# Four layers of attention and feed-forward: the two halves of the transposed scores exchanged, and the values matmuls moved up behind turns and projections

## The reference

```python
xn = _layernorm(x)
s = attention_l(xn, Wq, Wk, Wv, Wo)     # 32 heads of 16
g = _silu(ffn_l(xn, ...))
x = x + s * g
```

## Time and profile before

| | us |
|---|---|
| median of 3 runs (lowest, highest) | 1302.31 (1296.14, 1303.39) |
| the profiled execution | 1305.54 |
| its span, first to last instruction | 1303.8 |
| TensorE busy in it | 1166.5 (89%) |
| VectorE busy | 846.7 (65%) |
| ScalarE busy | 643.0 (49%) |
| GpSimd busy | 475.2 (36%) |

### The profile page before, as it was taken

One profiled execution on the slowest core, in us unless ns is written; L12 is line 12 of the kernel. 1 busy time (PEld: TensorE's weight loads), 2 busy tenths in 40 slices (PEclk: granted clock), 3 DMA queues, 4 the chain that ended last, 5 costly groups with the idle time before them and its releaser, 6 DMA issues.

```text
span 1303.8 us, 22325 instructions
## 1 busy us (share of the span) xinstructions
PE 1166.5 (89%) x8476; PEld 864.2 (66%) x8476; DVE 846.7 (65%) x1362; ACT 643.0 (49%) x1122; POOL 475.2 (36%) x636
## 2 busy tenths in 40 slices
PE   3999998988989898889999999998888888897897
PEld 3788876765656555555678787777666666675574
DVE  7743468876766656664655556537887778676453
ACT  3334357565454645544233433337756565565653
POOL 1000127454321111212444434406754465545542
PEclk9999989999999999959999999999999999999897
DMA  7000010110001000010243222201001001010001
GB/s 259 1 1 1 1 34 2 49 60 2 2 2 36 2 1 2 26 50 26 73 146 97 81 89 73 73 33 51 3 2 41 2 3 34 2 47 2 2 26 40
DMA packets 15260, 48.06 MB, mean 37 GB/s; under 512 B 2858, under 2 KB 6959, under 8 KB 14388
## 3 DMA queue, kind: packets, MB, share of 16 engines
q1 hardware_dynamic: 15156, 46.63, 10.6%
HBM read 44.00 MB, written 2.10 MB: 35 GB/s over the span
## 4 chain that ended last, share of the span: by engine, by line
PE 65%; DVE 14%; ACT 12%; issue 6%; DMA 1%; POOL 0%; POOLq 0%; ACTq 0%; DVEq 0%; SPq 0%
PE bank L662 18%; PE bank L778 14%; PE bank L692 8%; PE bank L906 8%; ACT probs L1364 6%; PE bank L881 5%; DVE negmax L1795 3%; PE bank L795 3%; PE bank L829 2%; ACT pv L1374 2%; PE bank L861 1%; PE bank L809 1%; DMA W_lo_whole<-in_w 1%; DVE stats L1452 1%; DVE W_lo_whole L1577 1%
## 5 line engine op out<-in xcount | busy, mean ns | idle before, releaser
L1795 DVE TENSOR_REDUCE negmax<-bank 128x4 f32<-128x1024 f32 (+1 forms) x256 | 250.1, 1016 | 89.1 <-PE bank L838 64.2
L1364 ACT ACTIVATE probs<-bank 128x1024 f32<-128x1024 f32 (+1 forms) x256 | 211.1, 863 | 33.1 <-PE bank L861 28.2
L2022 POOL TENSOR_SCALAR_AFFINE_SELECT probs<-probs 128x512 f32<-128x512 f32 x192 | 125.6, 673 | 122.6 <-ACT probs L1364 121.7
L1991 POOL TENSOR_TENSOR scaled<-pvT,recip 128x128 f32<-128x128 f32 x128 | 56.1, 439 | 289.1 <-DVE recip L1823 286.2
L1947 POOL TENSOR_TENSOR W_lo<-W_lo_whole,W_hi 128x1536 fp32r<-128x1536 f32 x28 | 98.4, 3517 | 117.2 <-ACT W_hi L1116 117.2
L829 PE MATMUL bank<-kT,qT 64*128 64x256 f32 (+1 forms) x1024 | 105.9, 302 | 25.1 <-DVE negmaxT L1813 10.3
L881 PE MATMUL bank<-probs,V 128*32 128x256 f32 (+1 forms) x2048 | 121.6, 356 | 3.1 <-DVE negmax L1795 1.7
L861 PE MATMUL bank<-qT,kT 64*128 64x256 f32 (+1 forms) x640 | 114.8, 388 | 6.0 <-DVE h_lo_whole L1623 3.1
L1374 ACT ACTIVATE pv<-bank 128x256 f32<-128x256 f32 x128 | 49.2, 384 | 135.5 <-PE bank L881 135.3
L829 PEld LDWEIGHTS bank<-kT,qT 64*128 64x128 f32 x1024 | 86.4, 194 | 44.2 <-issue 18.5
L1116 ACT ACTIVATE W_hi<-W_lo_whole 128x1536 fp32r<-128x1536 f32 x28 | 41.7, 1488 | 136.4 <-DVE W_lo_whole L1577 136.4
(11 more groups left out here) (203 smaller groups left out, 2697.1 us busy)
## 6 DMA issues: line engine op xcount, KB each, us to landing
W_lo_whole<-in_w SPq DMA_DIRECT2D x28, 768.0 KB, 4.2
Wqkv_lo_whole<-in_Wqkv SPq DMA_DIRECT2D x6, 768.0 KB, 6.5
Wo_lo_whole<-in_Wo SPq DMA_DIRECT2D x4, 1024.0 KB, 4.9
Wqkv<-in_Wqkv SPq DMA_DIRECT2D x2, 1536.0 KB, 7.3
Wdown_whole<-in_Wd SPq DMA_DIRECT2D x1, 2816.0 KB, 14.8
x<-in_x SPq DMA_DIRECT2D x4, 512.0 KB, 5.7
out<-x SPq DMA_DIRECT2D x8, 256.0 KB, 2.0
V_lo_whole<-in_V SPq DMA_DIRECT2D x1, 1408.0 KB, 6.5
```

What stands on the lines that cost most here:

```text
L1364: nc.scalar.activation(A[l].probs[gi % 2][kb][:, :, q0 - kb * A[l].probs1:].rearrange("p (b h) q -> p b h q", b=2), B.tensor(key)[:, :, 0: ...
L1795: v.tensor_reduce(A[l].negmax[u % 2][:, qb, :].rearrange("p (b h) -> p b h", b=2)[:, :, 2 * g:2 * g + 2], B.tensor(key)[:, :, 0:2 * nk].re ...
L2022: gp.affine_select(out=blk, in_=blk, compare_op=ALU.is_ge, fill=0.0, base=0, pattern=[[0, 4], [1, P]], channel_multiplier=-1).then_inc(cau ...
```

## The change

1. In each slot half 1 of the transposed scores comes first on TensorE, then the rows scores, then half 0. ScalarE takes the exponentials of half 1 first, GpSimd cuts half 1 first.
2. `QKV_BANK` becomes 6, so turned queries and projections use the banks of half 1; grouped keys go to bank 4 (shared with the rows scores), the values to bank 3 (shared with half 0) and, in the last slots of a run, to bank 6 in place of 4.
3. The values matmuls stand directly behind turns, projections and first feed-forward chunks, ahead of tile turns, output products, `turn_max`, `group_values`, `tile1` and `down`. Before, they closed every slot that had a filler.

```diff
-QKV_BANK = 2
-KEYS_BANKS = {True: (7, 1), False: (4, 2)}
+QKV_BANK = 6
+KEYS_BANKS = {True: (4, 1), False: (4, 2)}
 def values_bank(U, g):
-    return 6 if U + 2 + g % 2 < RUN else 4
+    return 3 if U + 2 + g % 2 < RUN else 6
 def scores_cols(l, u, g, kb):
-    if g == 0 and kb == 0:
+    if g == 0 and kb == 1:
         pe.wait_ge(m_rows[u % 2], 32 * (4 * l + u // 2 + 1))
 def slot(r, G):        # TensorE
-    scores_cols(l, u, g, 0)
+    scores_cols(l, u, g, 1)
     if G + LEAD < RUN * GROUPS:
         scores_rows(r, G + LEAD, 0)
         scores_rows(r, G + LEAD, 1)
-    scores_cols(l, u, g, 1)
+    scores_cols(l, u, g, 0)
...
-    if G >= 1 and not filled_out:
+    if G >= 1:
         weigh_values(r, G - 1, G)
     if tile_turned(U, g) is not None:
         transposes(2 * r + 1, (tile_turned(U, g),), banks=(NORM_BANK,))
     for n in rows_projected(r, U, g):
         project_out(*n, 1 if U % 2 == 1 else (4, 5)[n[2]])
...
-    if G >= 1 and filled_out:
-        weigh_values(r, G - 1, G)
 def slot(r, G):        # ScalarE
-    exponentials(r, G, 0)
     exponentials(r, G, 1)
+    exponentials(r, G, 0)
 def cut_future(r, G):  # GpSimd
-    for kb in range(2):
+    for kb in (1, 0):
```

More of the change, by code:

```diff
@@ L873, in weigh_values @@
                 else:
-                    pe.wait_ge(*B.emptied(("ST", l, u, g, 1)))
+                    pe.wait_ge(*B.emptied(("ST", l, u, g, 0)))
                 for tau in range(2):
@@ L915, in slot @@
                     scores_rows(r, G + LEAD, 1)
-                scores_cols(l, u, g, 1)
-                filled_out = False
+                scores_cols(l, u, g, 0)
                 if g == 0 and U + 1 < RUN:
                     turn_stacks(*unit(r, U + 1), 1)
-                    filled_out = True
                 if g == 2 and U + 2 < RUN:
                     turn_stacks(*unit(r, U + 2), 0)
-                    filled_out = True
                 if g % 2 == 1 and U + 3 < RUN:
                     project(*unit(r, U + 3), g // 2, QKV_BANK)
-                    filled_out = True
                 if r == 0 and (U, g) in PART2_SLOTS:
@@ L994, in ffn0 @@
                 turn_max(0, 0, 6)
-                turn_stacks(0, 1, 0)
+                turn_queries(0, 1, 0, 2)
+                turn_keys(0, 1, 0, 7)
                 scores_rows(0, GROUPS, 0, (4, 2))
@@ L1383, in slot @@
                 U, g = divmod(G, GROUPS)
+                exponentials(r, G, 1)
                 exponentials(r, G, 0)
-                exponentials(r, G, 1)
                 if g == 0 and U + 1 < RUN:
@@ L2162, in loads_0 @@
                 if U == 15:
-                    sp.wait_ge(*B.filled(("ST", 1, UNITS - 2, GROUPS - 1, 1)))
+                    sp.wait_ge(*B.filled(("ST", 1, UNITS - 2, GROUPS - 1, 0)))
                     load_chunk(2)
@@ L2191, in slot @@
                 if r == 0 and (U, g) == (15, 3):
-                    sp.wait_ge(*B.filled(("ST", 1, UNITS - 1, GROUPS - 1, 1)))
+                    sp.wait_ge(*B.filled(("ST", 1, UNITS - 1, GROUPS - 1, 0)))
                     load_chunk(3)
@@ L2215, in _ @@
                 slot(1, G)
-            sp.wait_ge(*B.filled(("ST", 3, UNITS - 1, GROUPS - 1, 1)))
+            sp.wait_ge(*B.filled(("ST", 3, UNITS - 1, GROUPS - 1, 0)))
             load(b2_whole[:], a["b2"], ffn3_in[2])
```

## The result

The kernel became slower: 1322.37 us, median of 4 runs (1318.60 to 1323.25), against 1299.22 (1288.94 to 1303.39) for the kernel before on the same chip, ratio 1.0192 with a 95% interval of 1.0152 to 1.0233. The forecast was 1307 in a range of 1291 to 1319: the side was missed too, since "within 0.5%" had the largest chance. The profiled execution took 1322.69 us, its span 1320.9, at a mean granted clock of 0.962; the other three runs had 0.961 to 0.966. Over all experiments the kernel before ran 84 times, median 1298.7, with a mean clock of 0.973 (0.963 to 0.987).

What follows compares the result with a forecast made beforehand. The prediction took TensorE, busy 89%, to be bound by its waits in the slots, chiefly for exponentials. Gains of 12.4 us and costs of 16.9 made net +4.5 on a median of 1302.3: 1306.8, say 1307, range 1291 to 1319.

Steps and rivals of the forecast that it cites:

- The exchange in plain causal units: Causal slots, short half first: gain of 0.2 us for g 2 and 3, 0.3 for g 0 and 1; 3.5 in all.
- The waits for exponentials: TensorE before turned queries (L795) and projections: waits fall from 21.4 to about 8 us and 23.0 to about 10.
- The chain behind the product at g 2: Product, residual, copy of maxima, rows scores all later: that wait grows from 10.3 to 18 us or more, near 1.4 in (3, 3).
- `tile1`: Layer 1, values ahead of this filler: tanh and gate lose their cover, six slots 0.6 us later, cost 3.6 (0 to 5).
- `group_values`: Layer 1, values ahead of this filler: first scale operation 1.0 us later, 0.54 reaches TensorE in three slots, cost 1.6.
- Layer 1's exchange: Layer 1, order of halves: both have 1024 columns, so the first exponential ends at the same time; gain 0.
- The turned keys in bank 4: Causal slots: keys wait for the first row maximum, which was said to be mostly done by then; no cost given.
- The costs of layer 1: Values ahead of small fillers there: `tile1` 3.6 us, `group_values` 1.6, tile turns at bank 5 1.0; 10.7 by the reflection's count.
- Values ahead of an output product, g 0: Causal units: the projection starts at 240.0 instead of 240.49, 0.6 us gained in each of 9 slots, 5.6 (3 to 6).
- Values ahead of an output product, g 2: Product ends later, so the next projection is mostly 0.7 us later a slot; cost 6.2 us (3 to 8).
- rival C: Idle over 1.4 us behind g 2 output products and `tile1` brings the lower clock: eight dips add 12 us, 1319; chance 0.17.
- B: Rival: VectorE and ScalarE waits hide half the costs (8.5 us arrive), some 7 of half-clock time returns; 1292, chance 0.23.

Runs made afterwards that it cites:

- e1: Changed kernel with the values matmuls back at the end of every slot that has a filler (exchange of halves and banks alone): 1293.1 us, ratio 0.9965.
- e2: Kernel before with the values matmuls moved early in every slot, halves and banks as before: 1323.8 us, ratio 1.0212.
- e7: Kernel before with one unused VectorE operation (0.65 us) added ahead of the copy of the turned maxima, g 2 of units 3, 5, 7: 1298.2 us, ratio 1.0004.
- e5: Changed kernel with the maxima turned ahead of the output product and copied ahead of the residual: 1318.7 us, ratio 1.0154 to the kernel before.
- e6: e1 with the values of each run's last slots in bank 4, as in the kernel before, not bank 6: 1291.4 us, ratio 0.9952.
- e8: e6 with the maxima turned ahead of the output product and copied ahead of the residual: 1281.6 us, ratio 0.9845.
- e9: e8 with bank 6 for the values of unit 13 of run 0 alone: 1282.3 us, ratio 0.9842.
- e11: Changed kernel with values early only in units 8 to 15 of run 0 (layer 1), late everywhere else: 1306.9 us, ratio 1.0046.
- e3: Changed kernel with values late, as before, in g 2 and in all slots with an output product: 1314.6 us, ratio 1.0104.
- e4: Changed kernel with values late in all slots without an output product and not of g 2: 1309.8 us, ratio 1.0096.
- e10: Changed kernel with values late in units 8 to 15 of run 0 (layer 1), early elsewhere: 1314.3 us, ratio 1.0101.
- e12: Changed kernel with values late only in the 16 slots with a tile turn: 1311.1 us, ratio 1.0110.
- e13: e8 with values early only in the 16 slots with a tile turn: 1297.6 us, ratio 0.9995.

## Why the prediction was wrong

**Where it failed, in short.** The sum gave +4.5 us and +23 were measured. The step that failed is the price of the values' earlier place: the forecast let the projection behind an output product gain 5.6 us (1.4 came), and put the tile turns of run 1, the turned keys, kstack and the lower clock at nothing. The forecast also started from 1302.3; the kernel before had 1299.2 with its fourth run.

**Right.** The exchange in plain causal units: 0.5 us a unit forecast, 0.55 measured ((2, 0) to (2, 3): +0.10, -0.43, -0.22, +0.01). The waits for exponentials vanish, and further than said (L795 to 3.4, not 8). The chain behind the product at g 2: 1.39 idle in (3, 3), 21.1 us in all where "18 or more" stood. `tile1`: its gate's waits are +4.6 us against 3.6, `group_values` +2.3 against 1.6. Layer 1's exchange: nothing in its slots at full clock (e1 within 0.03 us). Position costs, exchange pays: e1 and e2 show it.

**Failed: costs not in the sum.** Tile turns in run 1, +7.0 us of waits (9.4 less 2.4), were left out: I looked for what the values cover only behind products and in layer 1. Part comes back ahead of the turn, where the wait for the row maxima in bank 5 fell from 9.5 in e1 to 4.0. The turned keys in bank 4 behind the row maximum, called "mostly done", wait 5.6 us more; GpSimd's kstack, 3.8, was not looked up at all. These two come with the exchange (6.6 and 4.2 in e1), so they made its gain smaller. The costs of layer 1 were about right: 10.7 us in the sum, 11.4 in its slots at full clock.

**Failed: two terms mis-sized.** "Values ahead of an output product, g 0", a gain of 5.6: the projection was to start 1.4 behind the slot's start. It started 1.70 behind (240.03 less 238.33), because the rows scores wait 0.17 for the residual to free bank 1 and the scores themselves take 1.5. Slot (3, 1) gained 0.15, not 0.6, and nine such are 1.4 us. "Values ahead of an output product, g 2": 0.7 a slot forecast, (3, 2) and (3, 3) lost 0.47 + 0.91, of which about 0.4 is the exchange's (e1 has it in (3, 2)); 0.9 to 1.0 is the move's.

**Failed: the clock, put at nothing.** It was rival C's, at 0.17. C's time, 1319, is near the measured one by luck: it took 12 us for the clock on top of a 4.5 that was really 15 to 16, and its trigger is not borne out. By (1 - clock) x time, the most that half clock can cost is 35 us in the kernel before and 49 in the changed one, so 14 of the 23 us if both paid it in full; the line gives 8. The time at equal clock, not the clock, is the larger piece. The Trainium skill, "TensorE: Matmul & The Clock Gate", section "A second HAM failure mode: psum-queue depth-cycling", has small idles between groups of matmuls make the clock swing; by that rule the changed kernel should swing more. The trace agrees in the number of half-clock stretches, 19 against 13 in the whole profile, but e7 (more idle, 12 stretches) and e5 (less idle, the one in (4, 2) still there in both runs) show that the idle behind the maxima doesn't decide here.

**A slip in a rival.** B's sum, 1302.3 - 12.4 + 8.5 - 7, is 1291.4 and not 1289. Its mechanism did not come either: the lateness reached TensorE.

**Open.** What brings a half-clock stretch at a given slot. Shown is only their company. Between (3, 1) and (11, 0) of run 1 the seven profiles with the values late there (before, e1, e6, e7, e8, e9, e11) have 0 to 10 us at half clock, and eight of the nine with early values among them (the changed kernel twice, e3, e4, e5, e10, e12, e13) have 20 to 38. e2 is the ninth, with 10, and it is as slow as the changed kernel. An added idle of 0.6 us (e7) brought no lower mean clock. Each kernel but the changed one has a single profile, and stretches differ between executions, so single slots prove little. Open as well are some 10 us: waits and costs as listed don't add up to the 15 to 16 at equal clock, and e13's loss is larger than its waits and its clock.

## What to carry to other kernels

Before moving work from the end of a stage to its middle, list everything that stood in its shadow there: here 0.86 us of matmuls covered the emptying of whatever bank the filler ahead of it had filled, and it had to be costed for each filler, not for the most visible one. A wait that another wait covers is not a loss: e1 took away 28 us of waits for exponentials (44.4 to 16.5) and gained some 4.5. And compare two kernels at equal granted clock before putting a difference down to either. Order first what others wait for (the maxima ahead of the product), and keep as cover what nobody waits for (the values).

## What the runs showed of the hardware

Time goes with the granted clock. The same kernel ran from 1305 us at a clock of 0.977 to 1325 at 0.958 (e3), and over 84 executions of the kernel before 0.01 of clock went with 7.6 us. Between kernels with the same instructions the mean clock went from 0.961 (e5) to 0.977 (e9), some 12 us by that line. The stretches at 0.50 lasted from 3.4 to 23.9 us. Some recurred at the same slots, in a second execution of the changed kernel (four of six places) and in e10, whose slots of run 1 are the same; others did not.
